# A new plan for everything ahead of the second round: order of loads, x's statistics in two parts, integer casts on GpSimd, v's banks and slots, the output weights' own room

## The reference

```python
def xattn(x, context, ln_gamma, ln_beta, w_q, w_kv, w_out, b_out, gate):      # 16 heads of 64
    xn = layernorm(x, ln_gamma, ln_beta)
    q = (xn @ w_q).reshape(B, SQ, 16, 64)
    k, v = split(context @ w_kv, 2)                                            # 77 rows per batch
    attn = softmax(einsum('bqhd,bkhd->bhqk', q / 8, k))
    out = einsum('bhqk,bkhd->bqhd', attn, v).reshape(B, SQ, 1024)
    return (out @ w_out + b_out) * tanh(gate[0])
def ffn(x, w_gate, w_up, w_down):                                              # 768 hidden
    return (silu(x @ wg.T) * (x @ wu.T)) @ wd.T
x = x + xattn(layernorm(x), ctx_1024, ...)
x = x + ffn(layernorm(x), ...)
```

## Time and profile before

| What | Value |
|---|---|
| Runs | 337.5, 334.77, 336.14 us; median 336.14 us |
| Profiled execution, its own time | 335.7 us |
| Span of its records | 333.7 us |
| Mean granted clock of TensorE | 0.988 of full speed |
| TensorE matmul busy | 309.6 us (93%) |
| VectorE busy | 237.1 us (71%) |
| ScalarE busy | 170.4 us (51%) |
| GpSimd busy | 158.4 us (47%) |
| First matmul of the first T (round 0) | 70.02 us |
| First matmul of the second T (round 1) | 98.49 us |

### The profile page before, as it was taken

One profiled execution on the slowest core, in us unless ns is written; L12 is line 12 of the kernel. 1 busy time (PEld: TensorE's weight loads), 2 busy tenths in 40 slices (PEclk: granted clock), 3 DMA queues, 4 the chain that ended last, 5 costly groups with the idle time before them and its releaser, 6 DMA issues.

```text
span 333.7 us, 6358 instructions
## 1 busy us (share of the span) xinstructions
PE 309.6 (93%) x2419; PEld 281.2 (84%) x2419; DVE 237.1 (71%) x540; ACT 170.4 (51%) x322; POOL 158.4 (47%) x144
## 2 busy tenths in 40 slices
PE   7898687969997899999999999999999999989995
PEld 7896575847896889788988997899989889978994
DVE  2168979568776777678777778678787877785633
ACT  3455663456534662575267437724952683355032
POOL 1670054367620955096337806670963478045013
PEclk9999998999999799999999999999999999999999
DMA  5972414350415010301020121003010301100000
GB/s 174 383 260 53 138 54 172 131 178 0 176 55 157 1 40 0 96 0 40 3 95 2 38 64 32 14 27 96 0 40 1 97 0 40 51 14 0 17 19 31
DMA packets 16281, 23.28 MB, mean 70 GB/s; under 512 B 1602, under 2 KB 13866, under 8 KB 16250
## 3 DMA queue, kind: packets, MB, share of 16 engines
q1 hardware_dynamic: 15418, 22.72, 21.1%
q10 hardware_dynamic: 832, 0.13, 0.2%
HBM read 15.87 MB, written 4.62 MB: 61 GB/s over the span
## 4 chain that ended last, share of the span: by engine, by line
PE 63%; DVE 15%; DMA 11%; issue 4%; ACT 4%; SPq 1%; POOL 1%; POOLq 0%; DVEq 0%; ACTq 0%
DMA x_ln<-in_x 7%; PE ps L668 6%; PE ps L714 6%; PE ps L654 5%; PE ps L715 5%; PE ps L759 5%; PE ps L760 5%; PE ps L761 5%; PE ps L634 4%; PE ps L635 4%; PE ps L636 4%; DMA wk_raw<-in_L_xattn_w_kv 3%; PE ps L744 2%; PE ps L745 2%; PE ps L569 2%
## 5 line engine op out<-in xcount | busy, mean ns | idle before, releaser
L959 POOL TENSOR_TENSOR probs<-probs,total 128x616 f32<-128x616 f32 x32 | 38.7, 1219 | 89.6 <-DVE total L1081 89.6
L843 ACT COPY pt<-ps 77x512 f32<-77x512 f32 x64 | 34.0, 582 | 56.4 <-PE ps L654 54.4
L975 POOL TENSOR_TENSOR h_lo<-hid,h_hi 128x256 fp32r<-128x256 f32 x48 | 35.2, 739 | 40.0 <-ACT h_hi L897 39.9
L966 POOL TENSOR_TENSOR t_lo<-t_all,t_hi 128x1232 fp32r<-128x1232 f32 x16 | 45.6, 2851 | 7.8 <-ACT t_hi L864 7.8
L634 PE MATMUL ps<-t_hi,xn_hi 128*128 128x308 f32 x128 | 41.0, 320 | 0.4
L635 PE MATMUL ps<-t_lo,xn_hi 128*128 128x308 f32 x128 | 38.8, 303 | 0.0
L636 PE MATMUL ps<-t_hi,xn_lo 128*128 128x308 f32 x128 | 38.7, 303 | 0.0
L654 PE MATMUL ps<-ident,probs 128*77 128x128 f32 x256 | 34.3, 278 | 4.1 <-ACT pt L843 2.2
L759 PE MATMUL ps<-wo_hi,o_hi 128*128 128x256 f32 x128 | 36.0, 281 | 0.3 <-issue 0.3
L760 PE MATMUL ps<-wo_lo,o_hi 128*128 128x256 f32 x128 | 36.2, 283 | 0.0
L761 PE MATMUL ps<-wo_hi,o_lo 128*128 128x256 f32 x128 | 36.2, 283 | 0.0
(11 more groups left out here) (129 smaller groups left out, 842.8 us busy)
## 6 DMA issues: line engine op xcount, KB each, us to landing
x_ln<-in_x SPq DMA_DIRECT2D x11, 256.0 KB, 3.9
v<-v_scratch SPq DMA_DIRECT2D x8, 308.0 KB
v_scratch<-v_out SPq DMA_DIRECT2D x4, 512.0 KB, 2.7
stream<-in_x SPq DMA_DIRECT2D x8, 256.0 KB, 3.0
out<-stream SPq DMA_DIRECT2D x8, 256.0 KB, 2.2
wk_raw<-in_L_xattn_w_kv SPq DMA_DIRECT2D x4, 256.0 KB, 8.9
wq_raw<-in_L_xattn_w_q SPq DMA_DIRECT2D x1, 1024.0 KB, 8.9
wv_raw<-in_L_xattn_w_kv SPq DMA_DIRECT2D x1, 1024.0 KB, 10.6
```

What stands on the lines that cost most here:

```text
L959: nc.gpsimd.tensor_tensor(p, p, total[:, u, :].unsqueeze(2).to_broadcast([P, HG, K]), ALU.mult).then_inc(probs_done, 1)
L966: nc.gpsimd.tensor_tensor(t_lo[:, :, cols], t_all[:, :, n, cols], t_hi[:, :, cols].bitcast(F32), ALU.subtract).then_inc(tlo_done, 1)
```

## The change

All of it lies ahead of round 1. The work of the later rounds is the same, but for the place of a branch.

- **Loads.** SyncE issues the first part of w_k ahead of the context, and w_q after the other three parts. x of batches 0 to 3 follows, before w_v and the three integer matrices, and then batch 4. x has five rooms now (`x_ln` and four in `x_rooms`), in rising order of batches. The four small loads (gamma, beta, gate, bias) move from ScalarE's queue to SyncE's, behind all these. x_ln for batch 1 is loaded right after w_out, and no longer after v's stores.
- **w_k.** ScalarE makes the first `wk_hi` before it copies the context. The first half of k0 waits for three of the five context blocks only. Twelve warming matmuls become four.
- **Statistics in two parts.** Batches 0 to 3 are done one block at a time, after k2, w0, w1, k3, k4, w2 and VectorE's third and fourth `t` copy; XS follows for these. Batches 4 to 7 come in `DVE_START` (s4 to s7), and their scales (`XS2`) at the end of GpSimd's round 0.
- **t copies.** ScalarE takes 9 of 16, where it took 5 of 8.
- **Casts.** F0 to F2 move from VectorE to GpSimd, after XS and before its first Ta.
- **v.** The ten jobs take banks 4, 5, the free bank, 2, 3, 4, 5, the free bank, 4, 5. All are copied by ScalarE. The fifth block of rows takes slot 2 instead of slot 0. Each block has its own semaphore: C waits for the two blocks under `pt`, and ScalarE's first O for the others.
- **w_out.** `wo_raw` lies over `wqt_hi` now, so VectorE's O waits for it no more. WO on ScalarE and GpSimd moves from the start into round 0: behind X on ScalarE, behind P3 and B on GpSimd. The up weights go in place only after `wo_lo`, the down weights after XS2.
- **Flag.** The flag is made in the bank of XT at the end of the start, and TensorE's branch is moved from before round 0 to between rounds 0 and 1.

```diff
-PE_START = "v0 v2 v1 XT v3 v4 v5 FL S0 v6 S1 v7 v8 v9".split()
-ACT_START = "Ta X v3 v2 v1 v5 v4 Tb v6 E0 E1 WO".split()
-DVE_START = "F0 LN v0 F2 B0 F1 B2 B1 BC BR M0 M1 Z0 v7 v8 v9 Z1".split()
-POOL_START = "XS Ta X Tb P0 P1 WO".split()
-ACT_TS = "1 3 4 6 7".split()
-WARM_UP = (8, 12, 18, 6)
-STATS_PER_JOB = 2
+PE_START = "v0 XT v1 v2 v3 S0 v4 S1 v5 v6 v7 v8 v9 FL".split()
+ACT_START = "Ta X v0 v1 v2 v3 Tb v4 E0 v5 TG E1 v6 v7 v8 v9".split()
+DVE_START = "LN B0 B1 B2 BC M0 s4 M1 Z0 Z1 s5 s6 s7 BR BI".split()
+POOL_START = "XS F0 F1 F2 Ta X Tb P0 P1".split()
+ACT_TS = "1 3 5 6 8 10 12 13 15".split()
+STATS_AFTER = "k2 w0 w1 k3 k4 w2 t2 t3".split()
+V_BANKS = (4, 5, None, 2, 3, 4, 5, None, 4, 5)
+FIRST_X = 4
+WARM_UP = (8, 4, 18, 6)
...
-POOL_ORDER = "P2 Ta X P3 h0 B h1 h2 h3 Tb h4 h5 P0 P1".split()
+POOL_ORDER = "P2 Ta X P3 h0 B WO h1 h2 h3 Tb h4 h5 P0 P1 XS2".split()
...
-            wo_raw = sb("wo_raw", [P, IC, D], where=after_t)
+            x_rooms = sb("x_rooms", [P, 4 * NT, D], where=after_t)
...
+                if i == 1:
+                    sp.wait_ge(s_wol, 1)
+                if i == 2:
+                    sp.wait_ge(s_ln, 2 * X_STEPS)
...
                     for n2 in range(2):
                         cols = slice(n2 * HC, (n2 + 1) * HC)
+                        if i == 0:
+                            evacuated(pe, (HC - 1) // P if n2 == 0 else RC - 1)
...
                 if isinstance(b, int) and b == 0 and u == 1:
-                    pe.wait_ge(s_flag, 1)
+                    for n in range(first_v, last_v + 1):
+                        if V_BANKS[n - first_v] in (2, 3):
+                            evacuated(pe, n)
...
             start(PE_START, stages_of(False))
+            first_round(PE_ORDER, stages_of(False))
             pe.wait_ge(s_flag, 2)
             inexact_here = pe.value_load(inexact[0:1, 0:1])
             with pe.If(inexact_here > 0):
-                batches(pe, PE_ORDER, stages_of(True))
+                other_rounds(PE_ORDER, stages_of(True))
...
                         wait(act, pv_done, NU * b + 2 * g)
                         if isinstance(b, int) and b == 0 and g == 0:
-                            act.wait_ge(s_vrest, 16 * (RC - 1))
+                            for row in range(RC):
+                                if v_slot(row) < 2:
+                                    act.wait_ge(s_vrow[row], 16)
...
+            def to_float(i):
+                name, raw = (("wg", wg_raw), ("wu", wu_raw), ("wd", wd_raw))[i]
+                pool.wait_ge(s_in[name], 16)
+                nc.gpsimd.tensor_copy(raw[:], raw[:].bitcast(I32)).then_inc(s_float[i], 1)
```

More of the change, by code:

```diff
@@ L851, in copy_o @@
                         wait(act, proj_done, NT * b)
+                        if isinstance(b, int) and b == 0:
+                            for row in range(RC):
+                                if v_slot(row) >= 2:
+                                    act.wait_ge(s_vrow[row], 16)
                     nc.scalar.copy(o_hi[:, 2 * n:2 * n + 2, :],
```

212 lines of the change are left out of this document (117 added, 95 removed).

## The result

The changed kernel takes 323.35 us (median of four runs, 323.17 to 325.09) against 336.22 us: a ratio of 0.9627, 95% interval 0.9595 to 0.9658. The forecast was 324.5 us. The sum behind it was not right in the same measure: it said T of round 1 near 87 us and nothing gained behind it. All medians here leave out two executions that took several times as long as the rest (1657.51 us of near_branch, 1038.81 us of the kernel before).

The account below looks back on a forecast made before the run. TensorE is busy for 200.0 of 207.7 us from 126 us on, so gains lie ahead of it. 2.2 + 6.1 + 3.0 + 0.4 = 11.7 us, less 0.4 for handovers, gave 324.5 us (own range 322 to 327; wider 320.5 to 329.5).

Parts of the forecast that it names:

- Up to the first t job: Start until the first t job: earlier first k and a shorter hole for w_k's second part, together 2.2 us gained.
- Now that part is first: Start: w_k's first part loads ahead of the context, so the first k comes at 8.3 us, a gain of 1.8.
- The t jobs: t stretch: moving statistics from between VectorE's copies shortens it from 21.3 to 15.2 us, 6.1 gained.
- the v stretch: First v to first T: bank waits and slow pace go, 1.4 us of new waits come; 22.6 to 19.6, 3.0 gained.
- The casts' row: GpSimd in the v stretch: three casts at its measured cast rate take 1.43 us each, free up to 6.7 in all.
- 2.2 + 0.2 (its pipe) gained: Round 0, at C: it waits only for v's first two blocks, stored long before; 2.2 + 0.2 us gained.
- 1.7 us later: Round 0, at T3: the output weights' split on ScalarE delays the chain to T3 by 1.7 us.
- the branch: ... unhidden now, 0.3, with bounds of 0 and 0.9: Between rounds 0 and 1: load, compare and jump, no longer hidden, cost 0.3 us, with bounds of 0 and 0.9.
- Behind the last one nothing changes: From the first T of round 1 on: the later rounds take as long as before, so nothing is gained there.
- The casts were cheap: Rival for GpSimd's casts: at the subtraction's rate S0 starts 3.6 us late, 328 to 329.7 us in all; chance 0.17.
- x was not late among the k jobs: Rival for the k stretch: x lands with the last loads, 6 us lost, 330.5 us in all; chance 0.06.
- the clock did not fall at T3: Rival for round 0: T3's new wait slows TensorE's clock, costing 1.6 to 2 us, 326.3 in all; chance 0.10.

Follow-up runs that it names:

- near_branch: The changed kernel with the version of the rounds that is taken placed right behind TensorE's branch: 322.30 us.
- ctx_first: Against near_branch with x of batch 2 loaded ahead of the down weights' move: context loaded ahead of w_k's first part again; 317.74 us.
- the experiment: Against near_branch with x of batch 2 loaded early: early statistics pairs put behind copies t0 to t7 instead of among the k jobs; 321.38 us.

## Why the prediction was right, and where it was not

- **Up to the first t job** (2.2 forecast, 1.61 measured). The cause was half wrong. "Now that part is first" was given 1.8 us, and ctx_first shows it to be worth none: what let w_k's first part land early is the move of w_q or of the four small loads, and the sum gave 0.4 to the first and nothing to the second. The context's delay was sized well (6.2 against 6.28), the first k came 0.7 us later than forecast. The statistics among the k jobs cost nothing, as forecast: the k stretch is 15.53 us without a hole.
- **The t jobs** (6.1, measured 5.74) and **the v stretch** (3.0, measured 2.86): right in size. Of the t jobs' 5.74 us the experiment gives 1.74 to six of the fourteen pairs that moved; the other 4.0 are read from the trace (VectorE's copies as releaser before, hardly now) and were not taken apart. The same edit costs 1.27 us more by way of XS and the casts. In the v stretch the waits for a bank and the slow pace are gone (granted clock 1.00 instead of 0.92) and the two new waits are there as forecast (0.77 and 0.66); that the banks did it is read from the trace too. The casts' row, scaled by elements, gave 1.43; 1.47 was measured. The Trainium skill (GPSIMD Engine Reference, Elementwise) has two figures: the 1.8 cycles an element, from which 2.3 us were estimated, are its best case for larger loop bodies (k ≥ 3), and for the smallest (k ≤ 2) it states 1.03 cycles, an estimate of 1.3 us. The measured 1.47 us are nearer to the second.
- **Round 0.** "2.2 + 0.2 (its pipe) gained" at C is 2.0, "1.7 us later" for T3 is about nothing in the end; the round without its branch is 28.24 us and not 28.1. The step that failed is "the branch: ... unhidden now, 0.3, with bounds of 0 and 0.9". I took the upper bound from a gap of the kernel before which the branch shared with a copy, at a place where its jump may have been covered. It measured 3.65 us, and a T that was 0.9 us longer. The bound from the row was not a bound: it was measured in another place of the program, beside other work. Why the old place hid the jump was not tried. q8 shows two pieces there too, but the first moved at 66.4 us, 2.7 us before TensorE fell idle, and not 1.0 us after, and T waited only 0.87 us: the jump seems to have run beside v's last matmuls.
- **"Behind the last one nothing changes"** failed as well. The rounds behind it gave 5.1 us back: 3.1 in round 1, where x of batch 2 had come late and the branch's gap now covers that, and 3.35 in rounds 2 to 4, where pieces of code no longer meet x's load, less 1.3 in round 6. Against the 11.3 us of the sum, 7.06 were there at T of round 1: 1.1 short in the start and 3.55 in round 0, less the 0.4 taken off for handovers. The 5.1 us from behind made up for these 4.2. Round 1's share is no independent luck, as it is the branch's own gap in which x arrives: in near_branch, where the branch costs what the sum said, the total is 322.30 us, about 1 us less. The rest is luck of position. So the mechanism of the start held in the main, its total was 1.1 us short, and that the whole met 324.5 within 1.2 us was luck by some 4 us.
- **Rivals.** None of them was the missing one. The casts were cheap, x was not late among the k jobs, the clock did not fall at T3. One of the signs named for being wrong, "if T of round 1 starts after 91", came true (91.43), with a total inside the range.

## What to carry to other kernels

Where a branch has a body of thousands of instructions, put the version that runs right behind it: TensorE stood 3.65 us at a far jump here and 0.29 at a near one. By itself that gained nothing clear of the noise, for the next wait stood right behind. When a gap is taken away and the time stays, look in the next round for a load that the gap had covered, and move both. And before a loop's length is called fixed, look at how many us its small loads take to land in a short and in a long turn: a piece of the engine's own code that met them cost 0.8 to 1.4 us a turn here, and its place moved with the instructions added ahead.
